# Issuing the swaps of the first query chunk ahead of the reciprocal's round trip

## The reference

```python
x = x + attn(layernorm(x)); x = x + moe(layernorm(x))
proj = xn @ W_qkv                                  # 32 query heads, 8 key/value heads, head size 64
q, k = rope(q), rope(k)                            # halves of a head are swapped and multiplied by sin
attn = einsum('bqhmd,bkhd->bhmqk', q, k) / 8       # 4 query heads share a k/v head
attn = where((q_pos >= k_pos) & (q_pos < k_pos + 64), -inf, attn)
w = softmax(concat([attn, sink]))[..., :-1]
out = einsum('bhmqk,bkhd->bqhmd', w, v) @ W_out
```

## Time and profile before

| | before |
|---|---|
| median of three runs | 1159.13 us |
| the profiled execution | 1159.08 us |
| its span, first to last instruction | 1157.3 us |
| TensorE busy, share of the span | 1073.4 us, 93% |
| VectorE busy, share of the span | 879.1 us, 76% |
| GpSimd busy, share of the span | 726.1 us, 63% |
| mean granted TensorE clock | 0.979 |

### The profile page before, as it was taken

How to read it: one execution, slowest core, us unless ns; L and a number is a source line. 1 busy time by engine, 2 the same in 40 slices (tenths; PEclk the granted TensorE clock), 3 DMA queues, 4 the chain that set the end, 5 groups by cost and what they waited for, 6 DMA issues and landing times.

```text
span 1157.3 us, 30776 instructions
## 1 busy us (share of the span) xinstructions
PE 1073.4 (93%) x12411; PEld 727.2 (63%) x12411; DVE 879.1 (76%) x1912; ACT 641.4 (55%) x1515; POOL 726.1 (63%) x623
## 2 busy tenths in 40 slices
PE   4589999999999999999999999999984799999995
PEld 2345555555565555556555555655543799999995
DVE  6698888889888888988888889888873444444442
ACT  1355666666756666575566657556643344455451
POOL 5466666776666877766677776667622366666652
PEclk9989999999999999999999999999997799999998
DMA  8334543343343333333333233233323334344341
GB/s 216 138 106 114 150 119 103 105 114 87 97 127 84 94 85 94 88 96 114 99 92 88 75 95 109 75 83 96 109 62 104 126 92 107 98 105 106 98 105 19
DMA packets 116286, 117.94 MB, mean 102 GB/s; under 512 B 35184, under 2 KB 103856, under 8 KB 115248
## 3 DMA queue, kind: packets, MB, share of 16 engines
q1 hardware_dynamic: 108848, 107.43, 32.3%
q0 software_dynamic: 7296, 8.55, 4.4%
HBM read 77.31 MB, written 24.97 MB: 88 GB/s over the span
## 4 chain that ended last, share of the span: by engine, by line
PE 78%; DVE 15%; issue 3%; DMA 1%; POOL 1%; ACT 0%; SPq 0%; POOLq 0%; ACTq 0%; DVEq 0%
PE bank L1221 21%; PE bank L1202 21%; PE bank L1336 10%; PE bank L1176 9%; PE bank L1349 9%; PE bank L1234 5%; DVE probs_ring L942 4%; DVE probs_t L953 4%; DVE heads_sb L975 3%; PE bank L1314 1%; DVE xn L929 1%; PE bank L1183 1%; DMA swap_sb<-chunk_sb 0%; PE bank L1279 0%; POOL slot_rows L687 0%
## 5 line engine op out<-in xcount | busy, mean ns | idle before, releaser
L773 ACT ACTIVATE probs_ring<-probs_ring,neg_max 128x512 f32<-128x512 f32 x512 | 366.7, 717 | 271.6 <-DVE neg_max L942 269.7
L942 DVE CUSTOM_DVE_ANT_0 probs_ring<-bank,mask,sink_neg 128x512 f32<-128x512 f32 x512 | 364.9, 738 | 90.9 <-PE bank L1202 88.8
L953 DVE STREAM_TRANSPOSE probs_t<-probs_ring 128x1024 f32<-128x1024 f32 x256 | 317.6, 1241 | 0.0
L1202 PE MATMUL bank<-qk_st 64*128 64x512 f32 x1024 | 291.9, 647 | 15.5 <-DVE neg_max L942 13.9
L1221 PE MATMUL bank<-probs_t,v_quads 32*64 32x256 f32 x8192 | 246.9, 381 | 2.4 <-DVE probs_t L953 2.4
L1221 PEld LDWEIGHTS bank<-probs_t,v_quads 32*64 32x64 f32 x8192 | 178.7, 132 | 78.1 <-issue 48.1
L629 POOL TENSOR_TENSOR x_sb<-x_sb,y_sb 128x512 f32<-128x512 f32 x62 | 79.6, 1283 | 200.2 <-ACT y_sb L781 199.8
L1202 PEld LDWEIGHTS bank<-qk_st 64*128 64x128 f32 x1024 | 77.7, 186 | 110.7 <-issue 68.1
L609 POOL TENSOR_TENSOR chunk_sb<-chunk_sb,rope_sb 128x512 f32<-128x512 f32 (+1 forms) x96 | 123.1, 1283 | 32.2 <-DMA swap_sb<-chunk_sb 31.7
L1176 PE MATMUL bank<-xcur,w_hi 128*128 128x512 f32 x384 | 134.5, 432 | 2.2 <-DVE xcur L934 1.0
L1234 PEld LDWEIGHTS bank<-wo_sb,heads_sb 128*128 128x128 f32 x512 | 92.1, 189 | 58.4 <-issue 46.3
(11 more groups left out here) (136 smaller groups left out, 1465.6 us busy)
## 6 DMA issues: line engine op xcount, KB each, us to landing
v_quads<-v_rows SPq DMA_DIRECT2D x128, 128.0 KB
recip_wide<-recip_rows SPq DMA_DIRECT2D x64, 256.0 KB, 4.4
w_raw<-in_L_ffn_w SPq DMA_DIRECT2D x16, 1024.0 KB, 6.4
swap_sb<-chunk_sb SPq DMA_DIRECT2D x320, 32.0 KB, 2.1
w_raw<-in_L_attn_W_qkv SPq DMA_DIRECT2D x32, 256.0 KB, 3.2
slot_rows<-x2T SPq DMA_DIRECT2D x8, 662.5 KB, 5.3
slots<-slot_rows SPq DMA_DIRECT2D x8, 662.5 KB, 4.0
w_raw<-in_L_attn_W_qkv SPq DMA_DIRECT2D x64, 64.0 KB, 2.7
```

The lines of the kernel that those rows point to most:

```text
L773: nc.scalar.activation(probs[n % RING][:, :], probs[n % RING][:, :], ACT.Exp, bias=neg_max[j][:, n:n + 1], scale=-1.0, accum_out=sums[j][: ...
L942: nc.vector.tensor_tensor_reduce(probs[n % RING][:, :], SCORE[SCORE_OF[n // 2][n % 2]][:, :], mask[:, L - P - t * P:2 * L - P - t * P], -S ...
L953: nc.vector.transpose(probs_t[j][:, :, (h // 2) * (2 * P):(h // 2 + 1) * (2 * P)] .rearrange("p b (h q) -> p h b q", h=2)[:, :, :, t * BLK ...
L1202: nc.tensor.matmul(SCORE[SCORE_OF[n // 2][hh]][:, :], qk_st[j][half, h // 2, t * P:(t + 1) * P], qk_st[j][half, PAIRS, :], start=True, sto ...
```

## The change

In the loop over groups SyncE now issues the four swaps of Q01 before the reciprocals' round trip, not behind it:

```diff
             for g in range(GROUPS - 1):
                 swap_halves(g + 1, KV)
+                swap_halves(g + 1, Q01)
                 if g > 0:
                     recip_out(g - 1)
                     recip_spread(g - 1)
-                swap_halves(g + 1, Q01)
                 k_twice(g + 1, (g + 1) % 2)
```

## The result

| | before | after |
|---|---|---|
| median | 1159.55 us | 1197.2 us |
| ratio after / before | | 1.0317, 95% interval 1.0295 to 1.0338 |
| the profiled execution | 1159.08 us | 1202.17 us |
| its span | 1157.3 us | 1200.0 us |

One of the four timings after the change was 2364.63 us, twice the others (1195.24, 1196.14 and 1198.27), and the ratio leaves it out. The change costs 37 us. The forecast had the direction and the place, 1172.5, and too small a size; 1197.2 lies outside its range of 1160.5 to 1188.

What follows compares the result with a forecast made beforehand. The prediction took a TensorE chain passing through VectorE at L975 as the bound; stalls there of 11.3 + 0.6 us and 1.5 us of contention, 13.4 us on 1159.13, gave 1172.5 us, range 1160.5 to 1188.

Steps and rivals of the forecast that it cites:

- The place and the 1:1 passing on: At L975 VectorE stands on the path; whatever holds it there is passed on to TensorE 1:1.
- The issue step: On SyncE the first DMA of the reciprocals is issued at 462.86 instead of 457.01, 5.85 us later, behind four swaps.
- The first leg: First DMA of the reciprocals on SyncE: 1.44 us from its issue to the spread's in an ordinary group.
- the swaps hold the leg: Rival: Q01's four swaps delay the small write behind them, ordinary groups stall 0.9 us or more; 1186.5 us, chance 0.13.
- Late legs: First DMA of the reciprocals meets other traffic during TensorE's products with v: one group in three, each 1.1 us late.
- The spread: Second leg of the reciprocals, two DMAs: the last lands 4.9 us after issue, at 469.90 against L975 at 470.02.
- the traffic behind: `k_twice` and weights right behind the spread: bounds nothing to 0.5 us a group, taken as 0.1, 1.5 us in all.
- The sum: Stalls at L975 over 30 touched groups: 11.3 us in 21, 0.6 in nine, 1.5 for contention, together 13.4 us.
- the nine beside routing: Nine touched groups where Q01's copy is earlier against L975, 0.9 to 1.4 us more slack; 0.6 us of stalls.
- the slack already at 0.12: Time between the spread's forecast landing, 469.90, and L975 at 470.02; of 6 us nothing is left.
- What follows on SyncE: `k_twice`, the weights and v move behind the spread; their being later was costed at nothing.
- The gain: Q01's earlier swaps gain nothing, its rotation ending 6.95 us ahead of the scores that need it; bound 1.2 us.

Runs made afterwards that it cites:

- Run 3: The changed kernel with both legs of the reciprocals also behind the copy of k (`k_twice`); 1239.34 us, ratio 1.0677.
- run 2: The kernel before, with SyncE waiting for the copy of Q01 ahead of the reciprocals and Q01's swaps moved behind them; 1173.91 us, ratio 1.012.
- run 8: The changed kernel with 64 idle transposes ahead of TensorE's program, shifting its instruction blocks by half a block; 1205.11 us, ratio 1.0362.
- run 5: The changed kernel, but SyncE waits until the reciprocals' spread has landed before it issues the copy of k; 1204.36 us, ratio 1.0368.
- run 7: The kernel before, with only Q01's swaps moved late, behind the copy of k, and the reciprocals where they were; 1167.18 us, ratio 1.0046.
- run 4: The changed kernel with the loads of weights moved behind v's way out and in; 1203.28 us, ratio 1.0354.
- run 1: The changed kernel with the reciprocals' first leg back ahead of Q01's swaps, only the spread staying behind them; 1162.23 us, ratio 1.0013.

## Why the prediction failed in size

- **The place and the 1:1 passing on: right, and shown.** L975 waits, and 29 of 31 periods grew by their stop alone. Run 3 added 35.5 us of stops by a known delay and took 42 us, the surplus with the lower clock.
- **The issue step (5.85 us): short by 0.4.** In the mean of the ordinary groups it is 6.27, where 5.85 and 0.03 of reaction make 5.88. I took 2.46 us for four swaps, the value of one good group, where the mean over 30 groups was 2.63 us in the kernel before and is 2.73 after; some single swaps take 1.0 to 1.6 instead of 0.6 to issue. The copy of Q01 is 0.14 later too, nearly all of it from group 2. A mean was to be had, and the good group was used.
- **The first leg (1.44, late in one of three groups by 1.1): short by 0.4.** An undisturbed one takes 1.63 with four swaps right ahead of it and 1.45 without them (run 2), so the rival "the swaps hold the leg" was there, at 0.18 us and not at the 1.0 that it gave. Late legs came in 13 of 30 groups, not in a third, and by about 1.3 us, not 1.1. Their cause, instruction blocks of TensorE fetched during its products with v, is shown by run 8 for most of them. Here the rule of the Trainium skill (Runtime: NRT & Kernel Launch, Instruction fetch mechanics), that such a fetch is mostly hidden, is about the fetching engine, whose own cost no run here measures; for a neighbour's small DMA the runs have 1.3 us.
- **The spread: short by 0.3 to 0.4,** because of what was now issued right behind it. The budget has 4.9, but the stall was worked out with landings from 4.4 to 5.8, 5.1 in the mean, and it came at 5.4 to 5.5. The prediction had the traffic behind as a term of its own, with 0.5 as the upper bound, and took 0.1. Runs 5 and 8 put it at 0.5.
- **The sum, the step that failed.** It had 11.3 + 1.5 = 12.8 us of stalls in the 21 ordinary groups and 0.6 in the nine beside routing; measured are 31.1 and 4.7. Each of the three terms is short by a small amount, 0.3 to 0.4 us, together some 1.1 us a group. With the slack already at 0.12 they counted nearly in full in an ordinary group: an estimate from these differences is 21 x 1.1 = 23 us, the measured surplus 18.3, as a few groups still had slack. The terms were taken near their good ends, at the very point where the stall begins, and the range did not let the three go wrong together. The nine groups' greater slack, 0.9 to 1.4 us, was used up too in four of them.
- **What follows on SyncE: right.** `k_twice`, the weights and v cost nothing by being later: the periods without a stop at L975 kept their length.
- **The gain: right that there is none.** GpSimd's waits for swaps fell from 31.7 to 25.5 us and brought nothing. But the ground given was incomplete: the rotation has a nearer reader behind it on GpSimd, the gate arithmetic, as runs 2 and 7 show. Before the change that path had 1.1 us to spare in the group looked at (`top_gates` done at 343.41, its reader at 344.50).
- **The clock: not foreseen.** One place in the changed kernel: eight matmuls took 1.6 us longer, and the period grew by 0.5 us beyond its stop.

What stays open: what the stretched landing is worth in time by itself, since run 5 gave it back elsewhere, and what made run 4 slower than the changed kernel. No version beat the kernel before; its order meets both deadlines, and the nearest, run 1, is at 1.0013.

## What to carry to other kernels

On a queue that issues in order, a wait moved ahead of a two-leg transfer delays both legs, and a gap in which the queue would only have waited is the cheapest place for a DMA. When a change uses up a slack of 6 us to within 0.1, the stall is set by the spread of each term and not by its median, so take means over all groups and let them err together. And before calling a transfer early enough, look at what is queued behind its reader, not only at the reader's own result.

## What the runs showed of the hardware

- A 16 KB instruction block, fetched while a small DMA of 128 rows by 128 bytes is under way, made that DMA take 2.3 to 3.5 us instead of 1.6 (the changed kernel, 13 groups).
- Large DMAs issued directly behind a spread of 2 x 256 KB lengthened the landing of its second half from 4.9 us (run 5, with nothing behind) to 5.5 (run 8); four swaps of 32 KB behind it did not (run 2, 4.9).
- A stop of TensorE was followed by a granted clock of 0.50 in the changed kernel (a stop of 2.46 us) and in run 2 (1.93 us at the first place), and eight matmuls then took 3.5 to 3.6 instead of 2.0 us. Not each such stop was: behind one of 2.21 us in the changed kernel, up to 313.03, eight matmuls took 1.99 us as ever. After the longest stop in the changed kernel:

```profile
144.00:147.70 3.70, 1.24 (x6) 0.31 (x5) 0.82 (x3) 0.23 (x2) 1.98 (x2) 1.00 0.99 250
147.70:151.30 3.60, 3.60 (x10) 2.41 (x10) 3.60 (x8) 1.80 (x4) 0.00 (x0) 0.53 0.47 127
```

  In the first window TensorE was busy for a third of the time; in the second it worked throughout, at a mean of 0.53 of the clock. At such places the period grew by more than the stop: by 0.5 us here, by 1.7 us at the first place of run 2.
